# Value blocks of the first octet moved from the stage's start into slot 0; another order of ScalarE's copies and exponentials in slots without products

## The chip, the cores and the metric

The kernel runs on one core of a Trainium2 chip. The core has TensorE (PE, matrix products and transposes, with its weight loads PEld), VectorE (DVE), ScalarE (ACT), GpSimd (POOL) and SyncE (SP, which here only issues DMAs); each takes its instructions in the order in which they were written and waits on semaphores. The metric is the device time of one execution in microseconds. Before the change it is 1614.68 us, the median of three runs (1613.12 to 1619.3).

## The reference

Two layers over 64 batches of x (128 queries, 128 channels). Each is a gated cross attention to 77 context rows of the same batch and then a gated feed-forward part:

```python
x = x + tanh(g_xattn[0]) * L0_xattn(layernorm(x), ctx)        # ctx is (64, 77, 128)
x = x + tanh(g_ffn[0])   * L0_ffn(layernorm(x))               # 128 -> 512 -> 128, quantised, gelu
x = x + tanh(g_xattn[1]) * L1_xattn(layernorm(x), ctx, mask)
x = x + tanh(g_ffn[1])   * L1_ffn(layernorm(x))               # relu squared, 5 spiking steps

# each attention, 16 heads of 64
q, k, v = x @ Wq, ctx @ Wk, ctx @ Wv
attn = softmax(q @ k.T * 64 ** -0.5)                          # over the 77 keys
out = (attn @ v) @ Wo + bo
```

## The kernel before

Before an attention stage the weights are folded per head: A from Wq and Wk, B from Wv and Wo. A "key" product of a head is A times the context of a group of 4 batches (out 128 x 308, three matmuls in split precision). A "value" product is one block of context rows times B of four heads (out 128 x 512, three matmuls). The context rows of an octet of 8 batches are cut in five tiles of keys, each in four quarters of heads: 20 value blocks per octet (`BLOCKS`); there are 16 key products per group (`HEADS`).

A value block is copied from PSUM to a staging tile ST (a ring of six, `RING`), goes from there by DMA (`send`, L446) to a DRAM buffer, and comes back for each batch, laid out anew, as V (`fetch`, L457, five DMAs into a ring of three). A key product is copied from PSUM to G. A tile of ST is written again only when the DMA from it has landed (semaphore `sent`).

The stage (`attention`) is written as 65 slots, one per batch t and one to drain. In slot t TensorE makes products for later (`produce`: keys of the next group, value blocks of the next octet) and the scores of batch t in three units (`scores`), and it transposes and weighs the probabilities of batch t-1 (`turn_probs`, `weigh`). VectorE takes the row maximum and subtracts it (`row_max`, `shift`), ScalarE does the three exponentials (`exps`), VectorE the sum SM and its reciprocal RC, GpSimd multiplies (`normalise`, tile PN), TensorE transposes PN to pT, and ScalarE copies pT to PT (`probs_out`) for the weighing. `products(t)` lists the products of a slot; slots 60 to 64 have none. Products of slots go through two PSUM banks, pP0 and pP1, and ScalarE copies all of them.

Ahead of slot 0 stands a run of first products (L529 to L541 on TensorE): all 20 value blocks of the first octet, then the transposes of x of the first group (`turn_x`, bank pO), then the 16 keys of the first group. They go through four banks, pP0, pP1, pS0 and pS1; ScalarE copies the even ones and VectorE the odd ones. VectorE does the layer-norm statistics of the first group before its copies, and in layer 1 also the first two mask rows (`mask_bias`), which SyncE places in G by eight small DMAs (`place_mask`, L464) before it sends a value block. The order on every engine is the order of the code; no planner decides it.

Of the kernel before, what the change touches and what calls it, by code (L numbers as in the profile page):

```python
# [13 lines left out]
BATCH, QUERIES, KEYS, CH = 64, 128, 77, 128  # L14
# [8 lines left out]
KEYCOLS = GROUP * KEYS  # L23
# [10 lines left out]
RING = 6  # L34
# [311 lines left out]
def tile_rows(t):  # L346

    return 128 if t < TILES - 1 else PAIR * TAIL


def attention(nc, p, layer, ctx, ctx_dram, mask_dram):

    stats_after = layer == 0
    with ExitStack() as s:
# [57 lines left out]

        block = s.enter_context(nc.Block())

        FIRST = BLOCKS + HEADS
        OCTETS = BATCH // PAIR

        def products(t):

            keys = [("key", (t % GROUP) * 4 + j) for j in range(4)] if t // GROUP + 1 < GROUPS else []  # L420
            octet, n = t // PAIR + 1, t % PAIR
            start = octet * BLOCKS + sum(PLAN[:n])
            values = [("value", start + j) for j in range(PLAN[n])] if octet < OCTETS else []
            out = []
            for j in range(4):
                out += keys[j:j + 1] + values[j:j + 1]
            return out
# [11 lines left out]
        def _(sp):  # L439
# [28 lines left out]
            if layer == 1:  # L468
# [1 line left out]
                load_mask(1)  # L470
                place_mask(0)
                place_mask(1)
            for v in range(BLOCKS):
                sp.wait_ge(first_out[v % 2], v // 2 + 1)
                send(v)
            fetch(0)
            for t in range(BATCH):
                group, n = t // GROUP, MADE[t]
                if t % GROUP == 0 and group + CTX < GROUPS:
                    sp.wait_ge(ct_turned, group + 1)  # L480
                    load_context(sp, ctx, ctx_dram, group + CTX)
                if layer == 1 and t % GROUP == 0 and 1 <= group < GROUPS - 1:
                    sp.wait_ge(bias_ready, group)
                    load_mask(group + 1)
                if layer == 1 and t % GROUP == 1 and 1 <= group < GROUPS - 1:
                    sp.wait_ge(score_ready, group * 3 * GROUP)
                    place_mask(group + 1)
                if t % PAIR == 0 and t // PAIR >= 1:
                    for back in range(VRING):
                        last = t - 1 - back  # L490
                        sp.wait_ge(v_in[last % VRING], 16 * TILES * (last // VRING + 1))
                for kind, v in products(t):
                    n += 1
                    if kind == "value":
                        sp.wait_ge(made_out, n)
                        send(v)
                if t + 1 < BATCH:
                    fetch(t + 1)

# [2 lines left out]
        def _(pe):  # L502
# [23 lines left out]
                nc.tensor.matmul(out, hi, blo, start=False, stop=False)  # L526
                return nc.tensor.matmul(out, lo, bhi, start=False, stop=True)  # L527

            pe.wait_ge(tiled, 4 * CTX)  # L529
            pe.wait_ge(chi_out, CTX)  # L530
            pe.wait_ge(clo_out, CTX)
            for n in range(FIRST):
                if n == BLOCKS:
                    turn_x(0)
                wait(pe, first_out[n % 2], n // 2 - 1)
                if n < BLOCKS:
                    make_values(first_banks[n % 4], n).then_inc(first_made, 1)
                else:
                    make_keys(first_banks[n % 4], 0, n - BLOCKS).then_inc(first_made, 1)
            for i in range(2):  # L540
                pe.wait_ge(first_out[i], FIRST // 2)  # L541

            def slot(t):
# [55 lines left out]
                def weigh(n):  # L599
# [13 lines left out]
                    if n == 2:  # L613
                        last.then_inc(out_ready, 1)

                produce(0)
                produce(1)
                scores(0)
# [32 lines left out]
        def _(act):  # L651
# [12 lines left out]
                return nc.scalar.activation(ST[0:rows, v % RING, :], bank[0:rows, :], ACT.Copy)  # L664

            for n in range(0, FIRST, 2):
                if n == BLOCKS:
                    x_out(0)
                act.wait_ge(first_made, n + 1)
                if n < BLOCKS:  # L670
                    values_out(first_banks[n % 4], n).then_inc(first_out[0], 1)
                else:
                    keys_out(first_banks[n % 4], 0, n - BLOCKS).then_inc(first_out[0], 1)

            def slot(t):
                b, group = t % GROUP, t // GROUP
# [23 lines left out]
                def probs_out(n):  # L700
                    if prev:
# [3 lines left out]
                        if n == 0:  # L705
                            wait(act, out_ready, t - 1)
                        nc.scalar.activation(PT[0:rows, c0:c1, :], pT[n % 2][0:rows, 0:c1 - c0, :],  # L707
                                             ACT.Copy).then_inc(p_out, 1)

                produced(0)  # L710
                produced(1)
                produced(2)
# [3 lines left out]
                if b == 3 and cur and group + CTX < GROUPS:  # L716
                    act.wait_ge(ct_turned, group + CTX + 1)
                    act.wait_ge(tiled, 4 * (group + 1))
                    context_hi(nc, ctx, pO, group + CTX)
                produced(3)  # L720
                exps(1)
                produced(4)
# [12 lines left out]
        def _(dve):  # L735
# [52 lines left out]
            for n in range(1, FIRST, 2):  # L788
                dve.wait_ge(first_made, n + 1)
                bank = first_banks[n % 4]  # L790
                if n < BLOCKS:
                    rows = tile_rows(n // QUARTERS)
                    wait(dve, sent[n % RING], 16 * (n // RING))
                    nc.vector.tensor_copy(ST[0:rows, n % RING, :], bank[0:rows, :]).then_inc(first_out[1], 1)
                else:
                    nc.vector.tensor_copy(G[0:live, 0, :, n - BLOCKS, :],
                                          bank[0:live, 0:KEYCOLS].rearrange("p (b k) -> p b k", k=KEYS)
                                          ).then_inc(first_out[1], 1)

            def slot(t):  # L800
                b, group = t % GROUP, t // GROUP
# [879 lines left out]
```

## Time and profile before

| | us |
|---|---|
| median of three runs | 1614.68 |
| profiled execution | 1612.92 |
| its span, first to last instruction | 1610.5 |
| PE busy | 1447.8 (90%) |
| DVE busy | 1087.1 (68%) |
| ACT busy | 901.9 (56%) |
| POOL busy | 625.5 (39%) |

The mean granted clock of TensorE is 0.968 of full. The attention stage of layer 0 runs from about 29 to 631 us and that of layer 1 from about 800 to 1449 us; the feed-forward parts follow each.

A row of a timeline has the start, the length, the engine, the line, and the operation with out<-in by the program's names; the brackets hold the idle time of the engine just before it and what ended it. Several like instructions in a row are merged (x4). A score, or a step of the weighing, shows as two records.

### The profile page before, as it was taken

The numbers are of one execution on the slowest core, as the hardware profiler recorded it, in microseconds if no ns is written. First come the engines' busy times: TensorE is split into PE (matmuls) and PEld (weight loads), VectorE is DVE, ScalarE is ACT, GpSimd is POOL, SyncE is SP. The second block draws the span as 40 slices with busy tenths as digits, with TensorE's granted clock in tenths as the row PEclk, the third lists the DMA queues.
The fourth block names the chain that finished last, engine by engine and source line by source line (L and its number), as shares of the span: only waits on it lengthen the run. The fifth ranks groups of instructions, "written<-read, shape, count | busy, mean of one in ns | idle before, by whom it ended". The sixth has DMA issues, their size and how long they took to land. (4 is left out here: it accounts for less than half of the span.)

```text
span 1610.5 us, 27403 instructions
## 1 busy us (share of the span) xinstructions
PE 1447.8 (90%) x9094; PEld 1199.9 (75%) x9094; DVE 1087.1 (68%) x2372; ACT 901.9 (56%) x1903; POOL 625.5 (39%) x747
## 2 busy tenths in 40 slices
PE   6999999999999985559798999998999899977996
PEld 4888888888888874239777878787878787766774
DVE  5676676776767676898755656565656465666986
ACT  3666666666666653660155656565656565545662
POOL 1233434334334333840113333242423233337995
PEclk8999999999999998889899999999999999999998
DMA  8544444444443422000064444444444444310111
GB/s 247 185 154 134 141 152 131 159 131 155 132 153 130 143 79 81 18 0 0 18 205 131 134 128 134 131 135 132 137 132 133 128 130 139 91 58 4 31 33 40
DMA packets 198332, 182.30 MB, mean 113 GB/s; under 512 B 14144, under 2 KB 195392, under 8 KB 198208
## 3 DMA queue, kind: packets, MB, share of 16 engines
q1 hardware_dynamic: 197632, 180.60, 35.7%
q8 instruction: 68, 1.11, 0.3%
q14 instruction: 56, 0.46, 0.1%
q10 hardware_dynamic: 576, 0.13, 0.0%
HBM read 95.43 MB, written 84.93 MB: 112 GB/s over the span
## 5 line engine op out<-in xcount | busy, mean ns | idle before, releaser
L898 POOL TENSOR_TENSOR PN<-E,RC 128x512 f32<-128x512 f32 (+1 forms) x384 | 336.2, 903 | 587.7 <-DVE RC L855 587.7
L809 DVE TENSOR_REDUCE MX<-pS 128x6 f32<-128x462 f32 (+1 forms) x384 | 221.7, 577 | 263.8 <-PE pS L575 263.8
L610 PE MATMUL pO<-work,PT 128*128 128x128 f32 (+1 forms) x2560 | 332.8, 277 | 29.1 <-ACT PT L707 29.1
L658 ACT ACTIVATE G<-pP 128x308 f32<-128x308 f32 (+1 forms) x488 | 208.6, 428 | 244.5 <-PE pP L516 244.3
L610 PEld LDWEIGHTS pO<-work,PT 128*128 128x128 f32 (+1 forms) x2560 | 310.2, 192 | 37.4 <-issue 35.4
L575 PE MATMUL pS<-G,XT 128*128 128x462 f32 (+1 forms) x768 | 324.4, 507 | 0.0
L698 ACT ACTIVATE E<-E 128x462 f32<-128x462 f32 (+1 forms) x384 | 209.5, 546 | 153.6 <-DVE E L819 145.6
L514 PE MATMUL pP<-Chi,Ahi 128*128 128x308 f32 x496 | 240.1, 484 | 1.4 <-ACT G L658 1.2
L819 DVE TENSOR_TENSOR E<-pS,MX 128x462 f32<-128x462 f32 (+1 forms) x384 | 223.4, 582 | 9.1 <-issue 0.2
L707 ACT ACTIVATE PT<-pT 128x512 f32<-128x512 f32 (+1 forms) x384 | 200.5, 522 | 50.2 <-PE pT L595 50.2
L595 PE MATMUL pT<-ident,PN 128*128 128x128 f32 (+1 forms) x1280 | 202.8, 278 | 28.6 <-POOL PN L898 28.6
L853 DVE TENSOR_REDUCE SM<-E 128x16 f32<-128x1232 f32 x128 | 183.4, 1432 | 52.4 <-ACT E L698 52.2
L664 ACT ACTIVATE ST<-pP 128x512 f32<-128x512 f32 x290 | 171.9, 593 | 45.7 <-PE pP L527 40.5
L595 PEld LDWEIGHTS pT<-ident,PN 128*128 128x128 f32 (+1 forms) x1280 | 159.4, 141 | 49.8 <-issue 32.8
L525 PE MATMUL pP<-Bhi,Vhi 128*128 128x512 f32 x300 | 152.8, 509 | 11.2 <-PEq L145 9.2
L575 PEld LDWEIGHTS pS<-G,XT 128*128 128x128 f32 x768 | 136.1, 188 | 24.0 <-issue 6.4
L515 PE MATMUL pP<-Chi,Alo 128*128 128x308 f32 x496 | 151.1, 305 | 0.0
L516 PE MATMUL pP<-Clo,Ahi 128*128 128x308 f32 x496 | 151.0, 304 | 0.0
L514 PEld LDWEIGHTS pP<-Chi,Ahi 128*128 128x128 f32 x496 | 95.0, 191 | 35.3 <-issue 20.8
L526 PE MATMUL pP<-Blo,Vhi 128*128 128x512 f32 x300 | 120.7, 402 | 0.0
L527 PE MATMUL pP<-Bhi,Vlo 128*128 128x512 f32 x300 | 120.6, 402 | 0.0
L515 PEld LDWEIGHTS pP<-Chi,Alo 128*128 128x128 f32 x496 | 94.8, 191 | 32.2 <-issue 25.3
(197 smaller groups left out, 1958.0 us busy)
## 6 DMA issues: line engine op xcount, KB each, us to landing
values<-ST SPq DMA_DIRECT2D x256, 256.0 KB
work<-values SPq DMA_DIRECT2D x512, 128.0 KB
values<-ST SPq DMA_DIRECT2D x64, 208.0 KB
work<-values SPq DMA_DIRECT2D x128, 104.0 KB
C<-in_ctx SPq DMA_DIRECT2D x32, 154.0 KB
out<-s_O SPq DMA_DIRECT2D x16, 256.0 KB, 2.2
work<-in_L_xattn_Wq SPq DMA_DIRECT2D x2, 512.0 KB, 7.3
work<-in_L_xattn_Wkv SPq DMA_DIRECT2D x2, 512.0 KB, 7.9
```

The costliest lines, as they stand in the source:

```text
L514: nc.tensor.matmul(out, p["Ahi"][:, head, :], hi, start=True, stop=False)
L515: nc.tensor.matmul(out, p["Alo"][:, head, :], hi, start=False, stop=False)
L575: nc.tensor.matmul(out, XT[:, half, b, :], G[:, half, b, h0:h1, :].rearrange("p h k -> p (h k)"), start=True, stop=True).then_inc(score_re ...
L595: last = nc.tensor.transpose(pT[n % 2][0:rows, c - c0, :], PN[(t - 1) % 2][:, start:start + rows], p["ident"][:, :])
L610: last = nc.tensor.matmul(pO[:, 0:CH], PT[0:rows, c, :], V[(t - 1) % VRING][0:rows, tile, CH * hh:CH * hh + CH], start=c == 0, stop=c == C ...
L658: return nc.scalar.activation(G[0:live, g % 2, :, head, :], bank[0:live, 0:KEYCOLS].rearrange("p (b k) -> p b k", k=KEYS), ACT.Copy)
L698: nc.scalar.activation(e, e, ACT.Exp).then_inc(exp_done, 1)
L707: nc.scalar.activation(PT[0:rows, c0:c1, :], pT[n % 2][0:rows, 0:c1 - c0, :], ACT.Copy).then_inc(p_out, 1)
L809: nc.vector.tensor_reduce(MX[:, h0:h1], pS[u][:, 0:(h1 - h0) * KEYS].rearrange("p (h k) -> p h k", k=KEYS), X_AXIS, ALU.max).then_inc(max_ ...
L819: nc.vector.tensor_tensor(E[t % 2][:, h0:h1, :], pS[u][:, 0:(h1 - h0) * KEYS].rearrange("p (h k) -> p h k", k=KEYS), MX[:, h0:h1].unsqueez ...
L853: nc.vector.tensor_reduce(SM[:, :], E[t % 2][:, :, :], X_AXIS, ALU.add).then_inc(sum_done, 1)
L898: nc.gpsimd.tensor_tensor(out, e, scale, ALU.mult).then_inc(prob_ready, 1)
```

## The change

Three edits, in both layers. First, the run ahead of slot 0 holds only the 16 keys and then the transposes of x, and TensorE's waits at its start go down to the first context group. Second, in slot 0 TensorE does its three scores and then 27 products: the 20 value blocks of the first octet and the seven that the slot had. ScalarE copies all 27, with the three exponentials of batch 0 after the second, fourth and sixth. SyncE loads a context group, sends 23 blocks and fetches V of batch 0 after them. Third, in slots without products ScalarE does the first copy of PT before the second exponential, and the second and third copy before the third exponential.

```diff
--- before.py
+++ after.py
@@ -412,7 +412,7 @@
 
         block = s.enter_context(nc.Block())
 
-        FIRST = BLOCKS + HEADS
+        FIRST = HEADS
         OCTETS = BATCH // PAIR
 
         def products(t):
@@ -421,7 +421,7 @@
             octet, n = t // PAIR + 1, t % PAIR
             start = octet * BLOCKS + sum(PLAN[:n])
             values = [("value", start + j) for j in range(PLAN[n])] if octet < OCTETS else []
-            out = []
+            out = [("value", v) for v in range(BLOCKS)] if t == 0 else []
             for j in range(4):
                 out += keys[j:j + 1] + values[j:j + 1]
             return out
@@ -470,10 +470,6 @@
                 load_mask(1)
                 place_mask(0)
                 place_mask(1)
-            for v in range(BLOCKS):
-                sp.wait_ge(first_out[v % 2], v // 2 + 1)
-                send(v)
-            fetch(0)
             for t in range(BATCH):
                 group, n = t // GROUP, MADE[t]
                 if t % GROUP == 0 and group + CTX < GROUPS:
@@ -494,6 +490,8 @@
                     if kind == "value":
                         sp.wait_ge(made_out, n)
                         send(v)
+                if t == 0:
+                    fetch(0)
                 if t + 1 < BATCH:
                     fetch(t + 1)
 
@@ -526,17 +524,12 @@
                 nc.tensor.matmul(out, hi, blo, start=False, stop=False)
                 return nc.tensor.matmul(out, lo, bhi, start=False, stop=True)
 
-            pe.wait_ge(tiled, 4 * CTX)
-            pe.wait_ge(chi_out, CTX)
-            pe.wait_ge(clo_out, CTX)
+            pe.wait_ge(chi_out, 1)
+            pe.wait_ge(clo_out, 1)
             for n in range(FIRST):
-                if n == BLOCKS:
-                    turn_x(0)
                 wait(pe, first_out[n % 2], n // 2 - 1)
-                if n < BLOCKS:
-                    make_values(first_banks[n % 4], n).then_inc(first_made, 1)
-                else:
-                    make_keys(first_banks[n % 4], 0, n - BLOCKS).then_inc(first_made, 1)
+                make_keys(first_banks[n % 4], 0, n).then_inc(first_made, 1)
+            turn_x(0)
             for i in range(2):
                 pe.wait_ge(first_out[i], FIRST // 2)
 
@@ -613,6 +606,12 @@
                     if n == 2:
                         last.then_inc(out_ready, 1)
 
+                if t == 0:
+                    for u in range(3):
+                        scores(u)
+                    for j in range(len(todo)):
+                        produce(j)
+                    return
                 produce(0)
                 produce(1)
                 scores(0)
@@ -664,13 +663,9 @@
                 return nc.scalar.activation(ST[0:rows, v % RING, :], bank[0:rows, :], ACT.Copy)
 
             for n in range(0, FIRST, 2):
-                if n == BLOCKS:
-                    x_out(0)
                 act.wait_ge(first_made, n + 1)
-                if n < BLOCKS:
-                    values_out(first_banks[n % 4], n).then_inc(first_out[0], 1)
-                else:
-                    keys_out(first_banks[n % 4], 0, n - BLOCKS).then_inc(first_out[0], 1)
+                keys_out(first_banks[n % 4], 0, n).then_inc(first_out[0], 1)
+            x_out(0)
 
             def slot(t):
                 b, group = t % GROUP, t // GROUP
@@ -707,6 +702,12 @@
                         nc.scalar.activation(PT[0:rows, c0:c1, :], pT[n % 2][0:rows, 0:c1 - c0, :],
                                              ACT.Copy).then_inc(p_out, 1)
 
+                if t == 0:
+                    for j in range(len(todo)):
+                        produced(j)
+                        if j in (1, 3, 5):
+                            exps(j // 2)
+                    return
                 produced(0)
                 produced(1)
                 produced(2)
@@ -717,6 +718,13 @@
                     act.wait_ge(ct_turned, group + CTX + 1)
                     act.wait_ge(tiled, 4 * (group + 1))
                     context_hi(nc, ctx, pO, group + CTX)
+                if not todo:
+                    probs_out(0)
+                    exps(1)
+                    probs_out(1)
+                    probs_out(2)
+                    exps(2)
+                    return
                 produced(3)
                 exps(1)
                 produced(4)
@@ -788,14 +796,9 @@
             for n in range(1, FIRST, 2):
                 dve.wait_ge(first_made, n + 1)
                 bank = first_banks[n % 4]
-                if n < BLOCKS:
-                    rows = tile_rows(n // QUARTERS)
-                    wait(dve, sent[n % RING], 16 * (n // RING))
-                    nc.vector.tensor_copy(ST[0:rows, n % RING, :], bank[0:rows, :]).then_inc(first_out[1], 1)
-                else:
-                    nc.vector.tensor_copy(G[0:live, 0, :, n - BLOCKS, :],
-                                          bank[0:live, 0:KEYCOLS].rearrange("p (b k) -> p b k", k=KEYS)
-                                          ).then_inc(first_out[1], 1)
+                nc.vector.tensor_copy(G[0:live, 0, :, n, :],
+                                      bank[0:live, 0:KEYCOLS].rearrange("p (b k) -> p b k", k=KEYS)
+                                      ).then_inc(first_out[1], 1)
 
             def slot(t):
                 b, group = t % GROUP, t // GROUP
```

TensorE just before and in slot 0 of layer 0, before the change (Chi with Ahi or Alo: a key product; Bhi or Blo with Vhi or Vlo: a value product; G with XT: scores):

```order
L514 MATMUL pS1_0<-Chi_0,Ahi0 128x308
L515 MATMUL pS1_0<-Chi_0,Alo0 128x308
L516 MATMUL pS1_0<-Clo_0,Ahi0 128x308
L514 MATMUL pP0_0<-Chi_0,Ahi0 128x308
L515 MATMUL pP0_0<-Chi_0,Alo0 128x308
L516 MATMUL pP0_0<-Clo_0,Ahi0 128x308
L525 MATMUL pP1_0<-Bhi0,Vhi_0 128x512
L526 MATMUL pP1_0<-Blo0,Vhi_0 128x512
L527 MATMUL pP1_0<-Bhi0,Vlo_0 128x512
L575 MATMUL pS0_0<-G_0,XT_0 128x462
L514 MATMUL pP0_0<-Chi_0,Ahi0 128x308
L515 MATMUL pP0_0<-Chi_0,Alo0 128x308
```

After the change, from the last key on (pO from XN: the transposes of x):

```order
L512 MATMUL pS1_0<-Chi_0,Ahi0 128x308
L513 MATMUL pS1_0<-Chi_0,Alo0 128x308
L514 MATMUL pS1_0<-Clo_0,Ahi0 128x308
L506 MATMUL pO_0<-ident,XN_0 128x128 x4
L568 MATMUL pS0_0<-G_0,XT_0 128x462
L568 MATMUL pS1_0<-G_0,XT_0 128x462
L568 MATMUL pS2_0<-G_0,XT_0 128x308
L523 MATMUL pP0_0<-Bhi0,Vhi_0 128x512
L524 MATMUL pP0_0<-Blo0,Vhi_0 128x512
L525 MATMUL pP0_0<-Bhi0,Vlo_0 128x512
L523 MATMUL pP1_0<-Bhi0,Vhi_0 128x512
L524 MATMUL pP1_0<-Blo0,Vhi_0 128x512
```

The scores now stand directly behind the transposes of x, and the value products behind the scores, in pP0 and pP1 in turn.

ScalarE around the transposes of x in layer 0, before the change (ST: copy of a value block, XT: copy of the transposed x, G: copy of keys):

```order
L664 ACTIVATE ST_0<-pP0_0 104x512
L664 ACTIVATE ST_0<-pS0_0 104x512
L654 ACTIVATE XT_0<-pO_0 128x512
L658 ACTIVATE G_0<-pP0_0 128x4x77
L658 ACTIVATE G_0<-pS0_0 128x4x77
```

After the change (E0: exponential of batch 0):

```order
L657 ACTIVATE G_0<-pP0_0 128x4x77
L657 ACTIVATE G_0<-pS0_0 128x4x77
L653 ACTIVATE XT_0<-pO_0 128x512
L663 ACTIVATE ST_0<-pP0_0 128x512
L663 ACTIVATE ST_0<-pP1_0 128x512
L693 ACTIVATE E0_0<-E0_0 128x462
L663 ACTIVATE ST_0<-pP0_0 128x512
L663 ACTIVATE ST_0<-pP1_0 128x512
L693 ACTIVATE E0_0<-E0_0 128x462
L663 ACTIVATE ST_0<-pP0_0 128x512
L663 ACTIVATE ST_0<-pP1_0 128x512
L693 ACTIVATE E0_0<-E0_0 128x308
```

The copy of XT is now the last before slot 0, and ScalarE copies every value block in slot 0, with exponentials among them.

ScalarE in the last product-free slot with scores of layer 0, before the change (E1: exponential, PT: copy of transposed probabilities, the one of 104x256 being the third; the first row merges two exponentials):

```order
L707 ACTIVATE PT_0<-pT0_0 104x256
L698 ACTIVATE E1_0<-E1_0 128x462 x2
L707 ACTIVATE PT_0<-pT0_0 128x512
L698 ACTIVATE E1_0<-E1_0 128x308
L707 ACTIVATE PT_0<-pT1_0 128x512
L707 ACTIVATE PT_0<-pT0_0 104x256
```

After the change:

```order
L693 ACTIVATE E1_0<-E1_0 128x462
L702 ACTIVATE PT_0<-pT0_0 128x512
L693 ACTIVATE E1_0<-E1_0 128x462
L702 ACTIVATE PT_0<-pT1_0 128x512
L702 ACTIVATE PT_0<-pT0_0 104x256
L693 ACTIVATE E1_0<-E1_0 128x308
```

The third exponential is now the last of the slot, and the first copy of PT stands ahead of the second exponential.

## Rows read from the trace of the kernel before

**Rows 1.** Busy time by stretch; columns: span, then busy us per engine, TensorE clock, DMA share, GB/s

```profile
29.08:59.56 30.48, 29.84 (x139) 24.29 (x139) 17.12 (x41) 14.06 (x28) 2.30 (x2) 0.92 0.70 233
...
59.56:630.00 570.44, 554.69 (x3523) 464.96 (x3523) 402.88 (x938) 356.29 (x783) 214.94 (x270) 1.00 0.42 135
...
799.71:835.48 35.77, 32.15 (x139) 25.59 (x140) 19.17 (x48) 15.16 (x29) 2.33 (x3) 0.88 0.57 180
```

**Rows 2.** Timeline of TensorE, head of layer 0: start, us, instruction, idle before and releaser

```profile
45.26 0.60 PE L508 MATMUL pO<-ident,XN 128*128 128x128 f32 x4
...
45.61 0.39 PE L514 MATMUL pP<-Chi,Ahi 128*128 128x308 f32 x1
...
53.20 0.38 PE L514 MATMUL pP<-Chi,Ahi 128*128 128x308 f32 x1 [0.62 <-ACT G L658]
...
58.01 0.40 PE L525 MATMUL pP<-Bhi,Vhi 128*128 128x512 f32 x1
...
58.48 0.39 PE L527 MATMUL pP<-Bhi,Vlo 128*128 128x512 f32 x1
...
59.56 0.41 PE L514 MATMUL pP<-Chi,Ahi 128*128 128x308 f32 x1
...
66.63 1.05 PE L610 MATMUL pO<-work,PT 128*128 128x128 f32 x8
```

**Rows 3.** Timeline of ScalarE, head of layer 0

```profile
45.90 0.60 ACT L654 ACTIVATE XT<-pO 128x512 f32<-128x512 f32 x1 [0.53 <-PE pO L508]
...
58.91 0.60 ACT L664 ACTIVATE ST<-pP 128x512 f32<-128x512 f32 x1
```

**Rows 4.** Timeline of SyncE's queue, heads of both layers

```profile
48.94 3.32 SPq L457 DMA_DIRECT2D work<-values  x5
...
803.57 5.05 SPq L464 DMA_DIRECT2D G<-MB  x8
...
808.67 14.87 SPq L446 DMA_DIRECT2D values<-ST  x20
```

**Rows 5.** Timeline of VectorE, head of layer 1

```profile
804.79 0.67 DVE L794 COPY ST<-pP 128x512 f32<-128x512 f32 x1
```

**Rows 6.** Timeline of TensorE, head of layer 1

```profile
811.77 0.59 PE L525 MATMUL pS<-Bhi,Vhi 128*128 128x512 f32 x1 [2.33 <-ACT ST L664]
```

**Rows 7.** Busy time by stretch: after that stall, and in the product-free slots

```profile
597.00:612.00 15.00, 11.44 (x73) 8.88 (x72) 10.53 (x19) 5.76 (x12) 5.42 (x7) 1.00 0.28 85
...
811.80:815.20 3.40, 3.40 (x9) 2.59 (x10) 1.38 (x2) 1.11 (x2) 0.00 (x0) 0.53 1.04 342
```

**Rows 8.** Timeline of ScalarE, head of layer 1

```profile
831.41 1.28 ACT L698 ACT_TABLE_LOAD   x1
```

**Rows 9.** Timeline of VectorE, last slots of layer 0

```profile
604.39 0.64 DVE L809 TENSOR_REDUCE MX<-pS 128x6 f32<-128x462 f32 x1 [1.54 <-PE pS L575]
...
611.81 0.64 DVE L809 TENSOR_REDUCE MX<-pS 128x6 f32<-128x462 f32 x1 [1.54 <-PE pS L575]
...
619.35 0.58 DVE L809 TENSOR_REDUCE MX<-pS 128x6 f32<-128x462 f32 x1
...
623.43 1.44 DVE L853 TENSOR_REDUCE SM<-E 128x16 f32<-128x1232 f32 x1 [0.59 <-ACT E L698]
```

**Rows 10.** Timeline of TensorE, last slots of layer 0

```profile
608.31 1.13 PE L610 MATMUL pO<-work,PT 128*128 128x128 f32 x8 [1.78 <-ACT PT L707]
...
610.83 2.24 PE L575 MATMUL pS<-G,XT 128*128 128x462 f32 x6
...
621.77 0.63 PE L595 MATMUL pT<-ident,PN 128*128 128x128 f32 x4 [0.41 <-POOL PN L898]
...
623.20 1.13 PE L610 MATMUL pO<-work,PT 128*128 128x128 f32 x8 [0.79 <-ACT PT L707]
...
624.16 0.38 PE L595 MATMUL pT<-ident,PN 128*104 128x128 f32 x2
```

**Rows 11.** Timeline of ScalarE, last slot of layer 0

```profile
624.58 0.38 ACT L707 ACTIVATE PT<-pT 104x256 f32<-104x256 f32 x1 [0.69 <-PE pT L595]
```

## Prediction

> **What bounds the kernel now.** I read the busy time by stretch first, because the edit touches two heads and two tails of the attention stages. In layer 0's long middle TensorE is busy 554.69 of 570.44 us at full clock [rows 1]: there the order of the ScalarE copies is worth nothing, and the change does not touch it. The two heads (TensorE's first matmul of a stage up to the first product of slot 1) take 30.48 us in layer 0 and 35.77 us in layer 1 [rows 1], with the same 139 recorded matmuls, so layer 1 loses 5.3 us that layer 0 does not.
>
> Then the timelines. In layer 0 TensorE goes from values to the four transposes of x at 45.26 and to keys at 45.61; slot 0 starts at 53.20 after 0.62 us idle, for the copies of the last keys [rows 2]. Sixteen keys from 45.61 to 52.58 are 0.43 us each; a step of a value is 0.235 (58.01 to 58.48 is two), so a value is 0.70 of TensorE [rows 2]. Slot 0 ends with the product of 59.56: 6.36 us. In layer 1 SyncE issues eight mask rows from 803.57 for 5.05 us and only at 808.67 the first value block [rows 4]; the ring of six staging tiles fills, TensorE stands 2.33 us [rows 6], and comes back at the low level of its clock: 0.53 of full over the next 3.40 us [rows 7], so half of that is lost as well.
>
> In the four product-free slots before each stage's end the period is 7.42 us (604.39 to 611.81), VectorE waits 1.54 us for scores in each [rows 9], and TensorE waits 1.78 us for the first PT copy [rows 10], which stands on ScalarE behind the second exponential.
>
> **The change part by part: head of layer 0.** The work of TensorE stays the same; what counts is its idle time.
> - Removed: the idle time before 53.20, 0.77 with the refill of the array, and the stalls of slot 0. Its own work is 4 keys at 0.43, 3 values at 0.70 and three scores at 2.07 together (2.24 at 610.83, less 0.17 that overlaps what follows) [rows 10]. That is 5.85 of 6.36, so 0.5. Together 1.3 us.
> - Added, transposes: keys now come first, then x. XT is copied 0.64 us after the transposes start and takes 0.60 (45.26, 45.90) [rows 2, 3]. The scores stand right behind and wait for it: 1.3 us from the start of the transposes less their own 0.35 is 0.95 us idle.
> - Added, VectorE: it does statistics before its first copy, now of a key. TensorE reaches the sixth key sooner than it reached the sixth value: about 0.2 us.
> - Added, the run of products. Twenty value blocks went over four banks with ScalarE and VectorE in turn; now they go over two banks, and ScalarE copies all. One bank's loop is read in slot 0: product starts 58.01, its copy 58.91, 0.60 long [rows 3], next product in that bank 59.56 [rows 2]. That is 1.55 us; matmuls overlap (0.40 long at a step of 0.235), and a stall loses part of the 0.165 of overlap, 0.1 taken. So 1.65 for two values instead of 1.40: 0.125 lost a value, for the 18 that wait 2.2 us. Three exponentials lie between copies; the copies need 0.6 of each 0.82 us, so nearly all of that hides (0.1). Then four keys alternate with three values: each value holds the loop at 1.65 while TensorE has 1.13 to do, 0.5 for each of three pairs, and the first key of slot 1 waits likewise, 0.5. Sum 4.3 us, on 17.8 of work: 22.1. From below: no stall if the loop closes faster, 0. From above: three exponentials of a copy's 0.60 not hidden, 6.1.
> - Sum: 0.95 + 0.2 + 4.3 - 1.3 = 4.2 us slower, bounds -0.1 and 6.0.
>
> Of DMAs: fetch(0) moves behind 23 sends. Its five issues take 3.32 us [rows 4]; the data landed about 6 us after the first issue (estimate: issue plus what a transfer of this size needs at the 233 GB/s of the head [rows 1], 0.63 MB in 2.7 us). The last value of slot 0 is copied 0.05 us before slot 1 starts and its send goes first (0.4), so V is there about 6.4 us into slot 1, and the weighing stands 7.07 us in (59.56, 66.63) [rows 2]. I cost it at nothing; the cover is 0.7 us thin, and if it fails it costs up to 2 us a layer. Behind it SyncE has fetch(1) and three sends, not needed before slot 2. The waits dropped at the stage's start cost nothing and give nothing, since TensorE stands at the stage's barrier anyway; the context load, now ahead of the sends, adds one issue.
>
> **Head of layer 1.** The ring stall goes (2.33 us), and the low clock behind it (1.7), since nothing is sent while the masks are issued. What is late next is VectorE: it writes the two mask rows before its first copy, which starts at 804.79 [rows 5]. TensorE starts at 799.71 at low clock, five keys at about 0.77 (nine 512-column matmuls took 3.40 us at the low level [rows 7], 0.38 each, so 0.23 for 308 columns and 0.68 for three; twice 0.43 from above) bring it to 803.5, and the sixth needs that copy: it starts at 805.4, so about 1.8 us idle, where the old order had a longer product and no stall. Clock: either it rises at 805 as before or about 3.4 us later (the length of the stretch in rows 7), worth 1.5 us. From 805.4 eleven keys at 0.43, 1.3 for transposes and XT, 2.07 scores give 813.5; 22.1 for the products and a table load of 1.28 us [rows 8] that now falls between back-to-back copies give 836.8, or 838.3 with the late clock. Before it was 835.48: +1.3 or +2.8, I take 2.0; bounds -3.0 (no stall among products) and +4.6 (the exponentials unhidden).
>
> The Trainium skill (TensorE: Matmul & The Clock Gate, Part 1: The HAM clock gate) says that the default is the throttled state, activity releases it, and the observation is free-running, not reset when a kernel starts. The trace agrees in that the low level followed a stall; by that rule the 1.5 us could fall in either layer by phase alone. It also gives (ScalarE: Activation LUTs, What ACT_TABLE_LOAD costs) about 1.28 us for the load plus a drain of 1.38. The row shows the 1.28 alone; by the page the sum would be 1.4 us higher.
>
> **Tails.** With PT's first copy ahead of the second exponential TensorE's weighing starts 1.2 us sooner (608.31 to 607.1, right after the first exponential and the copy), which alone would make the period 6.2. But the third exponential now stands behind the third copy. In the last slot, first reduction 619.35: second transposes 621.77 (held by GpSimd), so weighing can start at 622.23 instead of 623.20; it takes 0.96 to the last transposes (624.16), and their copy comes 0.42 later (624.58) [rows 10, 11]. So that copy starts 4.26 us into the slot (0.38 long), the exponential behind it takes about 0.4, and the sum starts at 4.97 us into the slot, where it was 4.08 (623.43) [rows 9]. Sum 1.47, reciprocal 0.17: the new period is 6.61, set by VectorE. Slot 60 gives 0.89, slots 61 to 63 begin 0.89, 1.70 and 2.51 us sooner; the last slot gives 0.89 back, since its sum is what GpSimd and the end wait for. Layer 1: 2.51 - 0.89 = 1.6 us faster. Layer 0: slot 62 does statistics of X between the last shift and the sum, so it gains nothing: 1.70 - 0.89 = 0.8 faster. Bounds: each from 0 (third exponential takes all) to 1.2 x 4 = 4.8.
>
> **Sum.** 4.2 + 2.0 - 0.8 - 1.6 = 3.8 us slower. The profiled execution took 1612.92 us (span 1610.5), 1.8 below the median of three runs, 1614.68. So 1616.7 for such an execution and 1618.5 on the median's scale.
>
> **The rivals.**
> 1. ScalarE's loop does not bind the products (latency smaller when copies queue up). For it: ScalarE has 0.2 us of air per value. Against: 59.56 stands 0.05 behind the copy's end. Then layer 0 is -0.1 and layer 1 2.0 - 4.3 = -2.3, with the tails -4.8: 1609.9.
> 2. Slower than before: the many small stalls of two-bank products let TensorE's clock fall to the low level for the run. Place: the 27 products of slot 0. At the low level a value takes 1.13 (three of 0.38) to 1.40, say 1.3, not 0.82, a key 0.8 where pairs give 0.8 anyway: 23 x 0.48, about 11 us a layer, so +15 (one layer) or +26: 1629 to 1640. It decides once the stalls of the run weigh as much as those behind the 2.33 us stall. Against: in the product-free slots TensorE is busy 11.44 of 15.00 us with stalls of 1.78 us, and the clock stays at 1.00 [rows 7]; the run would be busier, 81 to 85%.
> 3. V of the first octet arrives late in slot 1, in both layers: +2 us each, 1622.5.
> 4. The third exponential behind the copies takes the whole gain of the tails: 1620.9.
>
> **How the numbers follow.** About 0.5% (8 us) is what a measurement of this kernel can tell from no change. Forecast 0.60, rival 1 0.17, rival 2 0.06, rivals 3 and 4 0.17. Only rival 2 is surely past +8 us; the upper bounds of both heads (6.0 and 4.6) with rival 3 and no gain in the tails come to +14.6, for 0.03 more. Past -8 us needs rival 1 with the tails at their upper bound, 0.05. So faster 0.05, same 0.86, slower 0.09. The range 1609 to 1625 takes in rivals 1, 3 and 4 and leaves rival 2 out.
>
> **What would show it.** In the profile after: the products of slot 0 in pairs of 1.65 us with a wait on ST's copies; TensorE idle about 1 us before the first score; no wait on the ring in layer 1, but one of 1.8 us on VectorE's copy near 803.6; a table load among the copies; slot 1 beginning at about 63.7 in layer 0; product-free slots of 6.6 us, with SM's wait longer than 0.59. It would be wrong if the pairs run at 1.40, if the clock falls in slot 0, or if the weighing of slot 1 waits for a DMA.

## The result, and the profile after

| | before | after |
|---|---|---|
| median | 1612.58 us (1610.31 to 1619.3, 20 runs) | 1620.6 us (1616.88 to 1626.81, 20 runs) |
| profiled execution, its span | 1612.92, 1610.5 | 1620.19, 1618.4 |
| mean granted clock | 0.968 | 0.966 |

The ratio is 1.0048 with a 95% interval of 1.0038 to 1.0058: 7.7 us slower (6.1 to 9.4), where +3.8 was forecast.

In one pair of traces TensorE's clock may fall in one and stay in the other by chance, so I cut every span at points that each kernel has: the first matmul of each attention stage, the first row maximum of slots 2 and 60, the end. A tail holds the last slots, the feed-forward part behind them and, in layer 0, the folding of layer 1's weights. Us in each piece (the kernels below the first two are the experiments; one profiled execution each):

| | L0 head | L0 middle | L0 tail, to next stage | L1 head | L1 middle | L1 tail, to the end |
|---|---|---|---|---|---|---|
| before | 42.08 | 525.82 | 202.73 | 47.38 | 568.14 | 195.27 |
| after | 46.65 | 525.71 | 204.73 | 49.37 | 569.92 | 195.64 |
| head_only | 47.26 | 525.73 | 202.71 | 50.84 | 570.32 | 195.51 |
| tail_only | 41.70 | 525.91 | 202.95 | 47.43 | 571.71 | 195.65 |
| tail_alt | 42.57 | 525.92 | 200.36 | 47.27 | 569.86 | 192.06 |
| after_banks | 43.81 | 525.78 | 202.91 | 46.89 | 567.34 | 195.21 |
| after_fetch | 46.29 | 525.59 | 203.59 | 48.81 | 574.19 | 193.37 |
| mask_behind | 41.23 | 525.81 | 202.54 | 43.59 | 566.47 | 195.71 |
| tail_warm | 42.55 | 525.81 | 203.56 | 47.42 | 569.26 | 193.20 |
| best | 43.41 | 525.70 | 201.59 | 48.58 | 570.58 | 193.71 |
| best_a | 42.23 | 525.81 | 200.15 | 43.66 | 568.72 | 193.50 |
| best_b | 42.12 | 525.79 | 200.06 | 43.66 | 570.46 | 191.75 |
| after_heads | 46.82 | 525.78 | 202.71 | 48.40 | 569.37 | 195.25 |

The untouched middle of layer 0 agrees within 0.33 us. That of layer 1 spreads over 7.7 us.

Busy time of after: the two heads up to slot 1's first product (they answer to [rows 1]), and the last slot of layer 0:

```profile
26.38:60.97 34.59, 32.72 (x139) 22.91 (x139) 12.38 (x38) 19.92 (x39) 5.96 (x6) 0.95 0.58 192
803.47:840.88 37.41, 32.93 (x139) 23.14 (x139) 13.93 (x40) 21.39 (x40) 5.94 (x6) 0.94 0.49 156
627.20:631.00 3.80, 3.68 (x18) 3.30 (x19) 0.00 (x0) 1.20 (x2) 1.49 (x2) 0.55 0.00 0
```

The heads grew from 30.48 to 34.59 us and from 35.77 to 37.41 [rows 1], with the same 139 matmuls. TensorE in the head of layer 0, after (it answers to [rows 2]):

```profile
35.24 0.60 PE L506 MATMUL pO<-ident,XN 128*128 128x128 f32 x4
36.62 2.31 PE L568 MATMUL pS<-G,XT 128*128 128x462 f32 x6 [0.78 <-ACT XT L653]
38.54 0.63 PE L523 MATMUL pP<-Bhi,Vhi 128*128 128x512 f32 x1
...
40.32 0.50 PE L523 MATMUL pP<-Bhi,Vhi 128*128 128x512 f32 x1
...
41.97 0.50 PE L523 MATMUL pP<-Bhi,Vhi 128*128 128x512 f32 x1
...
60.97 0.41 PE L512 MATMUL pP<-Chi,Ahi 128*128 128x308 f32 x1 [0.25 <-ACT ST L663]
...
68.39 1.16 PE L603 MATMUL pO<-work,PT 128*128 128x128 f32 x8 [0.40 <-DMA work<-values]
```

The scores wait 0.78 us for XT (0.95 forecast), and the pairs of values stand 1.65 us apart (40.32, 41.97), as forecast. The last row was not: the weighing of slot 1 stands 7.42 us into the slot (60.97 to 68.39) and waits for V of batch 0. ScalarE there, and SyncE in both layers ([rows 3, 4]):

```profile
39.67 1.29 ACT L663 ACTIVATE ST<-pP 128x512 f32<-128x512 f32 x2 [3.19 <-PE pP L525]
40.85 0.58 ACT L693 ACTIVATE E<-E 128x462 f32<-128x462 f32 x1
41.33 1.29 ACT L663 ACTIVATE ST<-pP 128x512 f32<-128x512 f32 x2
42.52 0.58 ACT L693 ACTIVATE E<-E 128x462 f32<-128x462 f32 x1
```

```profile
40.29 21.02 SPq L446 DMA_DIRECT2D values<-ST  x23
61.55 6.46 SPq L457 DMA_DIRECT2D work<-values  x10
...
818.95 22.27 SPq L446 DMA_DIRECT2D values<-ST  x23
841.46 6.39 SPq L457 DMA_DIRECT2D work<-values  x10
```

The exponentials fit between two pairs of copies. The fetch starts at 61.55, only behind the 23rd block. Head of layer 1, TensorE and ScalarE ([rows 6, 8]):

```profile
809.06 0.41 PE L512 MATMUL pP<-Chi,Ahi 128*128 128x308 f32 x1 [1.40 <-DVE G L799]
...
815.29 2.31 PE L568 MATMUL pS<-G,XT 128*128 128x462 f32 x6 [0.89 <-ACT XT L653]
...
822.06 0.50 PE L523 MATMUL pP<-Bhi,Vhi 128*128 128x512 f32 x1 [1.42 <-ACT ST L663]
...
848.20 1.16 PE L603 MATMUL pO<-work,PT 128*128 128x128 f32 x8 [0.31 <-DMA work<-values]
```

```profile
818.32 1.30 ACT L663 ACTIVATE ST<-pP 128x512 f32<-128x512 f32 x2 [3.29 <-PE pP L525]
819.64 1.28 ACT L693 ACT_TABLE_LOAD   x1
820.94 0.59 ACT L693 ACTIVATE E<-E 128x462 f32<-128x462 f32 x1
```

The ring stall of 2.33 us [rows 6] is gone; waits of 1.40 (VectorE's mask rows), 0.89 (XT) and 1.42 us (the table load) came. Last slots of layer 0, VectorE and TensorE ([rows 9, 10]):

```profile
605.22 0.58 DVE L812 TENSOR_REDUCE MX<-pS 128x6 f32<-128x462 f32 x1
...
611.82 0.58 DVE L812 TENSOR_REDUCE MX<-pS 128x6 f32<-128x462 f32 x1
...
619.30 0.57 DVE L812 TENSOR_REDUCE MX<-pS 128x6 f32<-128x462 f32 x1
...
624.27 1.44 DVE L856 TENSOR_REDUCE SM<-E 128x16 f32<-128x1232 f32 x1 [1.47 <-ACT E L693]
```

```profile
627.29 2.12 PE L588 MATMUL pT<-ident,PN 128*128 128x128 f32 x8 [2.49 <-POOL PN L901]
629.21 1.83 PE L603 MATMUL pO<-work,PT 128*128 128x128 f32 x8
...
631.09 1.50 PE L603 MATMUL pO<-work,PT 128*128 128x128 f32 x12
```

The period is 6.60 us instead of 7.42, and SM starts 4.97 us into the last slot, both as forecast. But eight matmuls of the drain take 1.83 us, where 1.06 is usual, and the clock there is 0.55 of full, near the low one of its two levels (1.2 and 2.4 GHz).

### The profile page after: what moved, and what is told of

It reads as the page before. It is cut to its first block and busy times, and to the rows that moved or that the text cites. A ratio compares the mean times of both kernels' runs of the same rounds, so it can differ in the third digit from the quotient of the medians.

```text
span 1618.4 us, 27441 instructions
## 1 busy us (share of the span) xinstructions
PE 1458.8 (90%) x9094; PEld 1201.3 (74%) x9094; DVE 1073.1 (66%) x2352; ACT 914.5 (57%) x1923; POOL 625.4 (39%) x747
## 5 line engine op out<-in xcount | busy, mean ns | idle before, releaser
L856 DVE TENSOR_REDUCE SM<-E 128x16 f32<-128x1232 f32 x128 | 183.4, 1433 | 63.8 <-ACT E L693 63.7
L663 ACT ACTIVATE ST<-pP 128x512 f32<-128x512 f32 (+1 forms) x320 | 189.7, 593 | 44.3 <-PE pP L525 39.7
L523 PE MATMUL pP<-Bhi,Vhi 128*128 128x512 f32 (+1 forms) x320 | 161.6, 505 | 4.5 <-ACT ST L663 4.2
L525 PE MATMUL pP<-Bhi,Vlo 128*128 128x512 f32 (+1 forms) x320 | 127.6, 399 | 0.0
L524 PE MATMUL pP<-Blo,Vhi 128*128 128x512 f32 (+1 forms) x320 | 127.5, 398 | 0.0
```

## The experiments

Each ran beside before. Changes in us are ratios, less one, times 1613, and are against before where nothing else is said.

**head_only**: after without the third edit.

```diff
-                if not todo:
-                    probs_out(0)
-                    exps(1)
-                    probs_out(1)
-                    probs_out(2)
-                    exps(2)
-                    return
```

> The kernel before with the first and second edit (keys first, value blocks behind the scores in slot 0) and without the third (ScalarE's order in product-free slots). Theory, from the comparison of the two traces: the heads cost 4.1 us in layer 0 and 1.6 in layer 1, and the weighing of slot 1 waits for V of batch 0, another 0.6 us in each layer: about +7 us against the kernel before. Rival (my prediction): the heads alone, +6.2, with no wait for V. In both the slots without products stay as before: period 7.4 us, VectorE waiting 1.54 us for scores, no stall of TensorE of over 2 us in the last slot.

Measured: 1620.81 against 1613.39, ratio 1.004 (1.0027 to 1.0054), +6.5 us. The medians don't part 7 from 6.2; the trace has the wait for V, a slot 1 (from its first row maximum to the next slot's) of 9.85 us in layer 0. Its layer 1 head is 1.5 us longer than after's: the low clock lasted past the sixth key (0.62 us instead of 0.41 for its first matmul at 807.90), the "late clock" of the prediction.

**tail_only**: before with the third edit, the same seven lines.

> The kernel before with the third edit alone. Theory: the last row maximum of each layer comes about 1.8 us (layer 0) and 2.5 us (layer 1) earlier, but the third exponential, now last, makes the sum SM wait 1.4 us more, and TensorE then stands 2.49 us for PN in the draining slot and comes back at the low level of its clock: of the gain about nothing is left in layer 0 (+0.3) and 0.8 in layer 1, together -0.5 us. Rival (my prediction): only the 1 us of the third exponential is given back, no fall of the clock: -0.8 and -1.6, together -2.4.

Measured: 1613.11 against 1613.39, ratio 0.9994 (0.9983 to 1.0004), -1.0 us. The idle time of 2.49 us and the low clock in the drain are there. The interval holds both -0.5 and -2.4.

**tail_alt**: before, with the third exponential ahead of the third copy.

```diff
+                if not todo:
+                    probs_out(0)
+                    exps(1)
+                    probs_out(1)
+                    exps(2)
+                    probs_out(2)
+                    return
```

> The kernel before; in slots without products ScalarE does first copy of PT, second exponential, second copy, third exponential, third copy. Theory: the third exponential is back before the third copy, so SM starts about 4.1 to 4.4 us into the slot instead of 4.97, PN is ready about 0.7 us sooner, TensorE's stall in the draining slot is under 2 us and the clock stays at its high level there; the period stays 6.4 to 6.8: -2 us or more in each layer, together about -5 against the kernel before and 4 less than the third edit alone. Rival: the fall of the clock in the draining slot has nothing to do with the stall for PN and stays, or the third copy, now later, holds the weighing back: together -2 or less.

Measured: 1607.4 against 1613.39, ratio 0.9965 (0.9952 to 0.9977), -5.6 us. TensorE and VectorE in the last slots of layer 0:

```profile
623.00 0.63 PE L595 MATMUL pT<-ident,PN 128*128 128x128 f32 x4 [1.61 <-POOL PN L905]
...
624.50 1.06 PE L610 MATMUL pO<-work,PT 128*128 128x128 f32 x8
```

```profile
615.89 0.58 DVE L816 TENSOR_REDUCE MX<-pS 128x6 f32<-128x462 f32 x1
...
619.97 1.44 DVE L860 TENSOR_REDUCE SM<-E 128x16 f32<-128x1232 f32 x1 [0.59 <-ACT E L698]
```

SM is back at 4.08 us into the slot, the period is 6.24, and both drains (the slot that only transposes and weighs the last batch) ran at full clock. What loses the tails is the place of one exponential. Some of it was luck in this trace: in best, with the same order and the same idle time ahead (1.61 and 1.75 us), both drains fell to the low level.

**after_banks**: after, with four banks in slot 0.

```diff
+        slot0_banks = pP + [b[:, :, :].rearrange("p a c -> p (a c)") for b in pT]
-                        wait(pe, made_out, m - 1)
+                        bank = slot0_banks[m % 4] if t == 0 else pP[m % 2]
+                        wait(pe, made_out, m - 3 if t == 0 else m - 1)
```

> The kernel after, but the 27 products of slot 0 go over four PSUM banks (pP0, pP1, pT0, pT1) instead of two. Theory: the pairs of value products take 1.65 us in both layers because product, copy and product share one bank; with four banks TensorE runs at 0.70 a value until ScalarE (27 copies and three exponentials) sets the pace: slot 0 loses 2 to 2.5 us, and in layer 1 about as much; 4 to 5 us less than the kernel after in all, part of it lost again because V of batch 0 is not sooner (its stores follow ScalarE's copies): 3 to 4.5 us less than after. Rival: ScalarE or the stores set the pace of slot 0, not the loop over a bank: less than 1.5 us in all.

Measured: 1614.72 against 1613.39, ratio 1.001 (0.9999 to 1.0021), +1.6 us, 6.1 below after by the two ratios. TensorE and, in layer 1, ScalarE:

```profile
42.35 0.39 PE L524 MATMUL pT<-Bhi,Vhi 128*128 128x512 f32 x1
...
43.04 0.40 PE L524 MATMUL pP<-Bhi,Vhi 128*128 128x512 f32 x1
...
43.74 0.40 PE L524 MATMUL pP<-Bhi,Vhi 128*128 128x512 f32 x1
```

```profile
832.13 0.60 ACT L665 ACTIVATE ST<-pT 128x512 f32<-128x512 f32 x1 [0.99 <-DMA values<-ST]
```

A value takes 0.70 us now: the loop over a bank was the bound. The gain is more than the 3 to 4.5 us expected; the heads of the table are 2.8 and 2.5 us shorter than after's, and the rest is not accounted for. What is late next is the staging ring, and slot 1 grows to 9.95 and 10.77 us, waiting for V.

**after_fetch**: after, with V of batch 0 fetched behind the 20th block.

```diff
                         send(v)
-                if t == 0:
-                    fetch(0)
+                        if v == BLOCKS - 1:
+                            fetch(0)
```

> The kernel after, but SyncE fetches V of batch 0 right behind the twentieth value block of slot 0 and not behind the twenty-third. Theory: the weighing of slot 1 waits for V (0.40 us in layer 0 and 0.31 in layer 1 in the trace of after, slots of 9.85 and 9.75 us against 9.16) because five fetches stand behind three blocks that SyncE must first wait for; the wait goes, slot 1 is 9.2 us again: 1.2 us less than the kernel after. Rival: the data themselves are late (the stores of the last blocks end just before), slot 1 stays at 9.7 or more: no change.

Measured: 1618.75 against 1613.27, ratio 1.0034 (1.0022 to 1.0047), 2.3 us below after by the ratios, too near for the intervals. The trace decides: slot 1 lasts 9.17 and 9.19 us and waits for no DMA. Both drains stayed at full clock here, although the idle time ahead of them was 2.49 us.

**mask_behind**: before, mask rows placed behind the sends.

```diff
                 load_mask(1)
-                place_mask(0)
-                place_mask(1)
             for v in range(BLOCKS):
                 sp.wait_ge(first_out[v % 2], v // 2 + 1)
                 send(v)
+            if layer == 1:
+                place_mask(0)
+                place_mask(1)
```

> The kernel before, but in layer 1 SyncE sends the twenty value blocks first and places the mask rows after them. Theory: the eight mask rows (5.05 us on the queue) are what filled the ring of staging tiles; without them TensorE's stall of 2.33 us in the head goes, and with it the low level of the clock over the next 3.4 us (another 1.6 us); the mask rows are back long before the first scores: about -4 us against the kernel before. Rival: the DMA engines, which move some 340 to 370 GB/s in that stretch, set the pace of the value blocks, and the stall only moves: less than 1.5 us; or the scores of slot 0 then wait for the mask rows: nothing gained.

Measured: 1611.6 against 1613.27, ratio 0.9994 (0.9985 to 1.0002), -1.0 us. Busy time in that head:

```profile
804.00:812.00 8.00, 8.00 (x36) 6.27 (x35) 3.46 (x5) 3.44 (x6) 0.00 (x0) 1.00 1.04 341
```

The stall is gone with the DMA engines fully busy (share 1.04), so the mask rows ahead of the blocks filled the ring, and the transfers did not. The head is 3.8 us shorter in this profile and in two more (43.59, 43.66 and 43.66 against 47.38). Why the median of this kernel shows only a quarter of that stays open; its runs spread over 10.2 us (1604.6 to 1614.8), and the profiled one was the fastest. In best_a, which adds tail_alt's edit, the two ratios (0.9945 and 0.9965) leave 3.3 us for the mask rows, with intervals that overlap.

**tail_warm**: tail_only, with spare products ahead of the drain.

```diff
                 weigh(2)
+                if t == BATCH - 1:
+                    pe.wait_ge(made_out, MADE[BATCH])
+                    for h in range(4):
+                        make_keys(pP[0], GROUPS - 1, h)
```

> The kernel with the third edit alone, and TensorE makes four key products that nobody reads (12 matmuls, 1.7 us) between the last weighing of slot 63 and the draining slot of each layer, where it would stand 2.49 us for PN. Theory: the stall was what brought the clock down; now the twelve last weighing matmuls and the transposes run at the high level, and the drain from the last row maximum to the last update of X is about 1.1 us shorter per layer than with the third edit alone: -2 to -2.5 us against it, and -3 against the kernel before. Rival: the clock falls all the same, because what TensorE does there is too little, or the fall was not tied to the stall: no gain, or a loss where the spare products delay the transposes.

Measured: 1611.16 against 1613.27, ratio 0.9989 (0.998 to 0.9998), -1.8 us.

```profile
622.61 0.30 PE L516 MATMUL pP<-Clo,Ahi 128*128 128x308 f32 x1
623.71 0.63 PE L595 MATMUL pT<-ident,PN 128*128 128x128 f32 x4 [0.80 <-POOL PN L909]
...
625.21 1.06 PE L610 MATMUL pO<-work,PT 128*128 128x128 f32 x8
```

From the first transposes to the last weighing it takes 4.11 us in both layers; in tail_only it took 5.75 and 5.09. From slot 60's row maximum to the last update of X that makes 1.6 and 1.0 us less than in tail_only. Layer 0's column of the table does not show it (203.56 against 202.95), since a stretch far behind, the folding of layer 1's weights, fell to the low level in this trace (see below). The medians of the two kernels differ by less than their intervals, and -3 was expected.

**best**: after with six changes.

```diff
+                if n == FIRST - 4:
+                    turn_x(0)
-            turn_x(0)
```

and likewise `x_out`; the two mask rows of VectorE at n == 3 and n == 9 of its copies; the edits of after_banks, after_fetch and tail_alt.

> The kernel after with six changes: slot 0's products over four banks; V of batch 0 fetched behind the twentieth block; the transposes of x before the last three keys; the two mask rows of VectorE behind its second and fifth key copy (layer 1); in slots without products the third exponential before the third copy of PT. Theory: against the four-bank version (+1.6 us to the kernel before): V's wait gone -1.5 to -2.4, the XT wait gone -1.9, TensorE's stall of 1.4 us for VectorE's first copy of layer 1 gone -1.4, the other order of the tails -4.6: together about -8 us against the kernel before. Rival: once TensorE is faster in slot 0 the staging ring (the stores) sets its pace, and V is no sooner there: -5 or less, all of it the tails.

Measured: 1609.9 against 1613.27, ratio 0.998 (0.9969 to 0.9992), -3.2 us: the rival. TensorE in slot 1 of layer 1:

```profile
839.48 2.07 PE L606 MATMUL pO<-work,PT 128*128 128x128 f32 x8 [2.48 <-DMA work<-values]
```

Slot 1 lasts 13.51 us, 4.3 more than in before: 2.48 are the wait for V, and the low level of the clock after it is in the rest (eight matmuls take 2.07 us and not 1.16). Faster products only reach slot 1 sooner; V comes when the stores have landed. By the table the heads still cost 1.3 and 1.2 us and the tails gain 1.1 and 1.8, though both drains fell to the low level (5.75 us) after only 1.61 and 1.75 us idle; that sum is not the 3.2 of the medians.

**best_a**: before with the edits of mask_behind and tail_alt.

> The kernel before with two changes: mask rows placed behind the twenty value blocks (layer 1), and in slots without products the third exponential before the third copy of PT. Theory: the two touch different stretches and add up. By the traces the first takes 3.8 us off the head of layer 1 (43.59 from the stage's first matmul to the second slot's end against 47.38) and the second 2.3 and 3.4 us off the two tails with what follows them: -9.5 us in the trace against the kernel before. By the medians (-1.6 and -5.9 alone) it is -7.5; I take -8.5. Rival: the measured gain of the first alone was 1 to 2 us only, because it is given back in the slots of layer 1 that wait for mask rows: then no more than -6.5.

Measured: 1602.65 against 1611.95, ratio 0.9945 (0.9923 to 0.9967), -8.9 us; the interval holds the rival's -6.5 too. **best_b** adds to it the spare products of tail_warm, with `range(2)`:

> The same two changes, and two spare key products (6 matmuls, 0.85 us) that nobody reads between the last weighing of slot 63 and the draining slot of each layer. Theory: with idle times of 1.6 to 1.75 us ahead of the drain its matmuls took 4.11 us in two of four cases and 5.75 in the others; with 0.8 us idle they always take 4.11: in the mean over runs 0.8 us less per layer, so 1 to 2 us less than without the spare products, and both drains of the profile at full clock. Rival: the clock in the drain is not tied to the idle time ahead of it: no difference, and a drain of 5.75 us can still be seen.

Measured: 1603.91 against 1611.95, ratio 0.9936 (0.9918 to 0.9954), -10.3 us. The intervals don't part the two. The drain of layer 1 in best_a and in best_b:

```profile
1434.49:1440.24 5.75, 5.34 (x30) 4.93 (x30) 0.00 (x0) 1.58 (x3) 1.40 (x2) 0.70 0.01 3
```

```profile
1437.14:1441.26 4.12, 3.71 (x30) 3.31 (x30) 0.00 (x0) 1.58 (x3) 1.40 (x2) 1.00 0.02 4
```

The same 30 matmuls take 1.63 us more at a mean clock of 0.70; TensorE stood idle 1.75 us ahead of them in best_a and 0.90 in best_b. Both kernels beat before and after: the first octet's values stay at the stage's start.

**after_heads**: after, with best's `turn_x` and mask rows alone.

> The kernel after with two changes in the run of keys: the transposes of x stand before the last three keys, and in layer 1 VectorE makes its two mask rows behind its second and fifth key copy and not ahead of the first. Theory: both waits are on the path. TensorE's 0.78 us (layer 0) and 0.89 us (layer 1) for the copy XT are hidden by three keys of 0.43 us, and its 1.40 us in layer 1 for the first G copy of VectorE goes: -3 us against the kernel after (+5 to the kernel before), if the table load (1.42 us of stall in layer 1) stays as it is. Rival: the scores then wait for the copy of the last key instead (0.6 to 0.8 us), and VectorE's key copies come late by the mask rows wherever these stand: -1 or less.

Measured: 1618.21 against 1611.95, ratio 1.0039 (1.0026 to 1.0053), 1.5 us below after by the ratios. Mostly the rival: the wait of 1.40 us falls to 0.20, but the scores now wait 0.62 us for the copy of the last key, where they had waited 0.78 and 0.89 for XT. The layer 1 head is 1.0 us shorter than after's, layer 0's no shorter.

## Why the prediction was right and where it was off

The sign was right and the median of 1620.6 us lies inside the range of 1609 to 1625, but the change was 4 us larger than forecast, twice its size. The terms of the sum, in the means of the table's rows that share an edit:

- **Head of layer 0, +4.2 forecast.** From the first matmul to slot 1 it is +4.11 (slot 1 begins at 60.97 and not at 63.7 only because the stage begins 2.70 us sooner): XT 0.78 for 0.95, VectorE's first key copy 0.16 for 0.2, pairs of 1.65 as worked out, no fall of the clock among the 27 products (1.00 from 38.54 to 60.97). Rivals 1 and 2 are out.
- **V costed at nothing, bound 2 us a layer: the step that failed.** The prediction had V there 6.4 us into slot 1 and the weighing at 7.07, and named this wait as a sign that it was wrong. V came at 7.42: the first fetch is issued 0.58 into the slot, behind a store, and the weighing that it releases starts 6.84 us later (61.55 to 68.39), not 6, with the five fetches of batch 1 in the same row. The price is 0.69 and 0.58 us (slots of 9.85 and 9.75 against 9.16 and 9.17), which after_fetch takes away. That is rival 3's mechanism at a third of its size. Head of layer 0 with it: 46.96 (after, head_only) less 42.07 (seven kernels with the old head) is +4.9.
- **Head of layer 1, +2.0 (+1.3 or +2.8).** It is +1.64 in after and 1.5 more in head_only with the late clock; with V, 50.1 less 47.38 is +2.7. VectorE's wait was 1.40 for 1.8, and the wait with the table load in it 1.42. Behind the load's 1.28 us the exponential starts at once (819.64, 820.94). The Trainium skill (ScalarE: Activation LUTs, What ACT_TABLE_LOAD costs) adds a drain of 1.38 us; the row does not show it.
- **Tails, -0.8 and -1.6: the other term that was off, by a cost left out.** The periods and the 0.89 given back came as worked out. (That SM starts at 4.97 to the hundredth is luck: the parts given for it, 4.26, 0.38 and about 0.4, add to 5.04.) From slot 60's row maximum to the last update of X, with full clock in the drain (after_fetch, tail_warm), it is 32.71 and 31.84 us against 33.63 and 33.57: -0.9 and -1.7. What I missed is that the late PN leaves TensorE 2.49 us idle before the drain, 0.57 before, and the low level then makes its 30 matmuls up to 1.64 us longer. Over five kernels with the third edit and three with the old order that stretch changes by +0.3 and -0.7: 0.4 faster and not 2.4. The whole columns (203.38 and 195.02 against 202.66 and 195.50) say 0.2 slower, because 0.7 us lie further on, in code that no edit touches.
- **Sum:** 4.9 + 2.7 - 0.4 = 7.2, inside the measured 6.1 to 9.4. Of the 3.4 us by which this is more than the forecast, 1.3 are V and 2.0 the tails. Rival 4, the tails' gain taken whole, nearly came true, half by its own mechanism (0.89 a layer) and half by the clock. With the whole columns the sum is 7.8, but that it meets the measured 7.7 is luck: the layer 1 middle is left out of it, and a part of it is chance.

The clearest such chance is in the layer 0 tail. The 32 matmuls that fold B for layer 1 took 3.8 us in after, after_fetch and tail_warm and 2.3 to 2.6 in the other ten kernels, and the stretch from the last update of X to the next stage 170.8 to 170.9 us there and 168.4 to 169.1 in the others. In after (clock 0.50 over these matmuls) and in before (1.00):

```profile
794.27 3.79 PE L246 MATMUL fold_bank<-w_hd_o,work 64*128 64x128 f32 x32
```

```profile
791.94 2.31 PE L246 MATMUL fold_bank<-w_hd_o,work 64*128 64x128 f32 x32
```

Not settled: whether the layer 1 middle, 1.8 us longer in after than in before, has anything to do with the change. I take it for luck, which is argued and not shown: it spreads from 566.5 to 574.2 over kernels, and the six kernels with the new head average only 1.1 us more than the seven with the old. The two extremes, mask_behind and after_fetch, differ by 4.2 us in what VectorE waits for mask loads (total, times, longest), but before and after wait alike (74.1 and 74.0), so the 1.8 us are something else:

```profile
DVE MB L741 <- DMA M<-in_mask_BxS_bf: 72.6, 14, 9.1
```

```profile
DVE MB L748 <- DMA M<-in_mask_BxS_bf: 76.8, 14, 9.7
```

## What to carry to other kernels

A run of products with little between them wants as many banks as the way from product to copy to next product needs: two banks cost 0.12 us a value here, four nothing, until the staging ring was late. When an engine's order is changed to start one thing sooner, ask what moved behind it: the last exponential, put behind a copy nobody was waiting for, turned -5.6 us into -1.0. And look at the idle time that a change leaves ahead of a short tail: besides itself it can cost what the clock takes. Before a sum of pieces is believed for meeting the median, compare the pieces that no edit touches.

## What the hardware showed

- **After equal idle time the clock falls in some drains and not in others.** Drains of 30 matmuls, all kernels and both layers: with 2.49 us idle ahead, eight of ten partly at the low level (5.1 to 5.75 us); with 1.61 to 1.75 us, three of six; with 0.57 to 0.90 us, none of ten (4.11 us). The fall was to the low one of the two levels. My own theory in tail_alt's expectation, that under 2 us is safe, fell with best (1.61 and 1.75 us). The Trainium skill (TensorE: Matmul & The Clock Gate, Part 1: The HAM clock gate) calls the observation free-running; that equal stalls end either way agrees with it.
- Where a stage starts varies in code that no kernel changed: the first matmul of layer 0's stage came between 26.38 and 29.16 us. In the two latest, before and best_b, TensorE had waited 1.79 and 1.74 us for a load of Wo; in after it had no such wait.
- The mask rows, eight small DMAs, cost SyncE's queue 5.05 us of issue. Ahead of large transfers that was worth 3.8 us; behind them (mask_behind) TensorE waits for none of it.
